# Moving the last stage of a sort from in front of a batch's local runs to behind its carries, on VectorE

## The reference, cut to what matters

```python
h = maximum(layernorm(x), 0)
for head in range(8):
    feat  = h @ W[head]                       # 6250 x 64
    logit = leaky_relu(alpha_s[src] + alpha_d[dst], 0.2)
    m     = segment_max(logit, src)           # over the edges of a source node
    e     = exp(logit - m[src])
    agg   = segment_sum(e / segment_sum(e, src)[src] * feat[dst], src)
x = x + relu(agg)                             # heads side by side
```

## Time and profile before

| | us |
|---|---|
| median of 3 runs (lowest, highest) | 2954.81 (2952.81, 2958.27) |
| the profiled execution's own time | 2949.85 |
| its span, first to last instruction | 2947.7 |
| PE, DVE, POOL, ACT busy in it | 2477.8, 2087.8, 1848.2, 1208.1 |

### The profile page before, as it was taken

How to read it: one execution, slowest core, us unless ns; L and a number is a source line. 1 busy time by engine, 2 the same in 40 slices (tenths; PEclk the granted TensorE clock), 3 DMA queues, 4 the chain that set the end, 5 groups by cost and what they waited for, 6 DMA issues and landing times. The chain is left out here.

```text
span 2947.7 us, 44087 instructions
## 1 busy us (share of the span) xinstructions
PE 2477.8 (84%) x10647; PEld 1532.7 (52%) x10692; DVE 2087.8 (71%) x3728; ACT 1208.1 (41%) x3972; POOL 1848.2 (63%) x1881
## 2 busy tenths in 40 slices
PE   5998479898898889898868888888888989999990
PEld 3565267676677677677656733333333333334440
DVE  8988678888988988888988565444444444445668
ACT  5943467777777677777745500000000000002220
POOL 0000267777777777777746367777777777774658
PEclk8999789999999999999989899999999999999995
DMA  6111478788888887888748867777777777773227
GB/s 210 60 49 41 123 223 243 236 243 234 238 242 235 240 234 239 235 239 241 234 148 261 299 196 210 210 210 210 210 209 210 209 210 210 210 210 119 66 57 298
DMA packets 243546, 589.44 MB, mean 200 GB/s; under 512 B 57744, under 2 KB 82832, under 8 KB 243400
## 3 DMA queue, kind: packets, MB, share of 16 engines
q0 software_dynamic: 133120, 443.52, 51.3%
q1 hardware_dynamic: 110280, 144.14, 14.9%
HBM read 533.43 MB, written 54.10 MB: 199 GB/s over the span
## 5 line engine op out<-in xcount | busy, mean ns | idle before, releaser
L557 POOL DMA_INDIRECT big<-feat_table,idx x880 | 850.0, 966 | 631.0 <-ACT idx L582 337.2
L1210 POOL DMA_INDIRECT big<-h_table,idx x784 | 742.0, 946 | 306.2 <-issue 269.9
L608 ACT ACTIVATE big<-big,late_weights 128x65 f32<-128x65 f32 x2640 | 644.9, 340 | 0.0
L870 PE MATMUL psA<-big,onehot 128*128 128x260 f32 x1760 | 437.4, 392 | 10.4 <-issue 1.5
L870 PE MATMUL psB<-big,onehot 128*128 128x260 f32 x1760 | 431.5, 388 | 4.3 <-DVE acc L753 0.5
L582 ACT CAST idx<-late_keys 128x8 int32 (+1 forms) x101 | 20.1, 203 | 944.9 <-DMA big<-h_table,idx 944.9
L870 PEld LDWEIGHTS psA<-big,onehot 128*128 128x128 f32 x1760 | 317.8, 190 | 93.0 <-issue 51.6
L870 PEld LDWEIGHTS psB<-big,onehot 128*128 128x128 f32 x1760 | 317.0, 190 | 56.4 <-issue 10.0
L1651 DVE TENSOR_TENSOR acc<-acc,psCD 128x512 f32 x176 | 120.5, 684 | 210.3 <-PE psCD L1966 208.2
L1651 DVE TENSOR_TENSOR acc<-acc,psA 128x512 f32 x176 | 120.5, 685 | 203.3 <-PE psA L1966 200.6
L1965 PE MATMUL psCD<-big,onehot 128*128 x352 | 185.1, 607 | 50.1 <-ACTq L1366 47.3
(11 more groups left out here) (465 smaller groups left out, 3796.1 us busy)
## 6 DMA issues: line engine op xcount, KB each, us to landing
nodes_all<-slot_nodes SPq DMA_DIRECT2D x56, 512.0 KB
big<-feat_table,idx POOLq DMA_INDIRECT x880, 3.9
feat_table<-big SPq DMA_DIRECT2D x49, 264.0 KB, 2.1
x_table<-acc SPq DMA_DIRECT2D x49, 256.0 KB, 5.9
h_table<-big SPq DMA_DIRECT2D x49, 256.0 KB, 3.9
big<-h_table,idx POOLq DMA_INDIRECT x784, 3.7
big<-h_table SPq DMA_DIRECT2D x49, 256.0 KB, 2.6
big<-x_table SPq DMA_DIRECT2D x49, 256.0 KB, 4.1
```

The lines of the kernel that those rows point to most:

```text
L557: g.indirect_dma_start(ring[:, b.k, q * SB + u, :], None, feat_table, bass.IndirectOffsetOnAxis(ap=idx[:, 2 * b.k + q, u:u + 1], axis=0)). ...
L608: ins = s.activation(part, part, ACT.Copy, scale=late_weights[:, at:at + 1])
L870: ins = pet.matmul(psum[:, 512 * hf:512 * hf + HALF_W], onehot[:, q, u % SB, :], ring[:, b.k, u, HALF_W * hf:HALF_W * (hf + 1)], start=(u ...
L1210: g.indirect_dma_start(big[:, place:place + D], None, h1_table, bass.IndirectOffsetOnAxis(ap=idx[:, r.c % CHUNK_CYCLE, b:b + 1], axis=0)). ...
```

## The change

The last stage of the list of each pass (the second of two, or the only one) is taken from behind `add_lot(this, 3)` and stands between `make_onehotT(aft, 1)` and `find_tops(nxt)` at a = 5. No instruction is added or taken away.

```diff
@@ -778,6 +778,8 @@
                             carry_runs(nxt)
                         if a == 5:
                             make_onehotT(aft, 1)
+                            if this and late.stages.get(this.c):
+                                late_stage(*late.stages[this.c][-1])
                             find_tops(nxt)
                             make_factors(nxt)
                         if a == 7:
@@ -787,7 +789,7 @@
                         add_lot(this, a, tiles[a % LOTS])
                         if a + 1 == LOTS:
                             tiles = load_tiles(dve, tileA, this(2, 1))
-                            for j, step, at in late.stages.get(this.c, ()):
+                            for j, step, at in late.stages.get(this.c, ())[:-1]:
                                 late_stage(j, step, at)
```

## The result

The changed kernel takes 2960.43 us (median of 15 runs, 2957.37 to 2965.47), against 2954.81 us before (15 runs). The ratio is 1.0025, with a 95% interval from 1.0017 to 1.0032. The forecast was 2934 us with a range from 2920 to 2948, so it failed in size and in sign. The profiled execution takes 2958.01 us (before: 2949.85), its span is 2956.0 us, 8.3 more than before; the medians are 5.6 us apart.

A forecast was written before the change was run, and what follows sets the result against it. One chain of DVE and PE was taken to set the pass, with POOL taking over after the change. Gain 17 + 3.2 + 0.95 = 21 us from a median of 2954.8 gives 2934 us, range 2920 to 2948.

The forecast's parts named there:

- In front of the local runs: Without the second stage there, local runs and all behind them come 1.21 us earlier in 36 two-stage passes.
- Behind the one-hots: Moved stage fills DVE's idle before L712, delaying the rest 0.2 to 0.4 us; net gain 0.95 us a two-stage pass.
- The stage's own place: The stage before find_tops outlasts DVE's idle there and delays find_tops, lot 5's add and lot 7: 0.3 us charged.
- What POOL allows: POOL's 16 gathers a pass, 20.3 to 20.4 us, take over as the loop's limit and cap the gain at 21 us.
- The waits: POOL's real waits between gathers from 410 us on, beyond 0.30 us a gap: 17 us that can be gained.
- The lead and the last pass: POOL's gathers land 3.2 us early, usable once; the last pass with stages gains 0.95 us after POOL's last gather.
- What the moved stage does to POOL: Sum of gather extensions under DVE work, 13 to 17 us in the loop, stays; no change taken.
- the bound of 17: Worst case for gather extensions in the loop: they double, costing 17 us more.
- Both signs: Forecast is wrong if two-stage passes stay near 20.9 us or gathers lengthen by more than 0.03 us each.
- rival D: No change: the wait at L843 goes straight to another place, for instance L839; 2952 to 2958 us, chance 0.05.
- rival E: Slower: the moved stage's two instructions each catch a gather at its start for 0.5 us; 2970 us, chance 0.06.
- the point of decision: Longer gathers make the kernel slower from 0.58 us more a two-stage pass (21 / 36).

The follow-up runs named there:

- Experiment 1: One gather in 16 left out of both kernels from batch 2 on: kernel before 2955.14 us (ratio 1.0016), changed kernel 2907.39 us (0.9855).
- experiment 2: Kernel before plus two extra DVE minima where the changed kernel has its moved stage: both operands from SBUF 2962.67 us, one from PSUM 2957.44 us.
- experiment 6: Changed kernel with only the last stage's maximum moved, minimum left before the local runs, one-hots ahead of lot 4's add: 2932.51 us (0.9938 to kernel before).
- woven: Changed kernel with the moved stage's minimum ahead of the add of lot 4 and its maximum behind the one-hots: 2952.36 us (1.000 to kernel before).
- onehots_apart: Changed kernel with the one-hots ahead of the add of lot 4, which reads PSUM: 2948.67 us (0.9988 to kernel before).
- experiments 4: Changed kernel with only the last stage's maximum moved, its minimum staying in front of the local runs: 2937.85 us (0.9958 to kernel before).

## Why the prediction was wrong, step by step

**In front of the local runs: right.** PE's wait at L843 went from 56.9 us to 1.3.

**Behind the one-hots: right in kind, too small.** The net gain of a two-stage pass was put at 0.95 us, at most 1.05. Experiment 1 measures 1.27, and 47.7 us in the loop instead of 34. The stage's own place was charged at 0.3 us; the gain is larger than the whole 1.21 us in front of the local runs, so that charge wasn't due.

**What POOL allows: right.** POOL took over, its waits went to nothing, and ACT began to wait for landings. The waits were put at 17 us and were 15.1: from 410 us on the gaps less 0.30 us a gather fall from 19.1 us to 4.0 by this row.

```profile
L557 POOL DMA_INDIRECT big<-feat_table,idx x836 | 833.5, 997 | 254.8 <-issue 228.6 <-PE psA L872 16.8 <-PE psB L872 9.4
```

The lead and the last pass were put at 3.2 + 0.95 = 4.15 us. From the end of the last gather to the loop's end it was 16.55 us (1484.92 to 1501.47) and is 12.47 (1497.89 to 1510.36), 4.1 less.

**What the moved stage does to POOL: the step that failed.** "I expect the sum of these extensions to stay ... I take no change, being in the middle of the two." The sum did not stay. Gathers took 26.8 us more, beyond the bound of 17 that I had given it, because I had read the middle of two bounds as if it were evidence. The stated range did not even hold that bound: 2934 + 17 is 2951. With that one term at its measured size the sum is -17 - 3.2 - 0.95 + 26.8 = +5.7 us, with the waits at their 15.1 too it is +7.6, and the loop measured +7.6. The other 0.7 of the span's 8.3 lie ahead of the loop (+1.3) and behind it (-0.6). Both signs that the prediction had named for a wrong forecast were there: two-stage passes near 20.9 us (21.01), and gathers longer by more than 0.03 us (0.031). The first was put down to rival D, and it came from POOL's longer gathers.

This is the mechanism of rival E, at a lower price: it was given 0.58 us a two-stage pass as the point of decision and 1.0 as its own, and came to 26.8 / 36 = 0.74. It isn't two catches of 0.5 us in each pass, as E had it, but some 39 more catches in all, of up to 1.4 us each. It had a chance of 0.06. Its argument against, that a mean of 965 ns shows such catches to be rare, held only for the layout of the kernel before. The stage there stood behind another stage, from SBUF alone as well, and was mostly met at harmless moments: 22 gathers started 0.11 to 0.14 us ahead of its maximum and took 1.01 to 1.04 us. Here it stands behind the one-hots, and the gathers meet it at the moments listed with the result.

**What is shown and what is open.** Shown: the gathers set the loop (experiment 1), the second SBUF operand lengthens them (experiment 2), and the same work laid out otherwise costs them nothing extra (experiment 6 against the changed kernel). The traces also show that within one layout the moment of a gather's start goes with its length. Open: the rule behind it, and why the minimum ahead of the add holds gathers for so long in `woven`. Neither the length of a run nor a gap in front of it orders all the kernels by their gathers. No experiment sets the phase between the two engines by itself.

## What to carry to other kernels

A slot in which an engine idles is free only if nobody else needs what the engine holds while it works. Where GpSimd issues indirect DMAs at full rate, price a DVE instruction whose inputs are all in SBUF by the time that it can hold a gather, and look in the trace for the moment at which gathers start under it. Parting such instructions by one that reads PSUM helped in `onehots_apart` and in experiment 6 and not in `woven`, so each order has to be measured. When a forecast says that another engine takes over as the bound, that engine's own durations are the next term to look at, and its range belongs into the answer's range in full. Moving half of the work (experiments 4 and 6) can be worth more than moving all of it.

## What the runs showed of the hardware that was not expected

A gather can be held for the whole of a gapless row of DVE instructions, 1.4 us here (2.37 against 0.94), and cutting them into pieces doesn't let it in (1001 ns against 996). One that starts at another moment is let in at the first end of an instruction (1.36 us). Some 10 ns may decide: gathers that start 0.11 to 0.14 us ahead of a maximum take 1.01 to 1.04 us in the kernel before, and those that start 0.08 to 0.10 us ahead of the moved one take 1.58 to 1.60 in the changed kernel. The two maxima stand in different places, so the 10 ns are what these rows suggest and not shown by themselves.

TensorE's clock: in pass 27 PE stood 3.60 us at L841 for a late gather. Lot 4's eight matmuls behind it then took 3.68 us where the other lots take 1.92 to 2.02, and the pass had a granted clock of 0.86 (the loop 0.98, before 1.00). It was 0.50 from 959 to 964 us, the lower level of 1.2 GHz, after PE had stood idle from 955.5 to 959.1. POOL had no waits in that pass, so the loop's length as a sum of gathers holds without this; the slow lots are a sign of late gathers, not a second cause. That they shift the phases is possible and wasn't tried.
